# Two transformer layers on one core: VectorE's separate increments after its own writes are removed

## The reference

```python
x = layernorm(x + attn0(x))   # 16 heads of 8; q and k are divided by their row norms; softmax(q k / (8 * temperature)) v, projection
x = layernorm(x + ffn0(x))    # rows quantized to int8 by their absolute maximum, times int8 weights, scaled back, plus a bias
x = layernorm(x + attn1(x))   # 16 heads of 8; q and k normalized per head, rotated by position; causal softmax; projection
x = layernorm(x + ffn1(x))    # silu(x Wg) * (x Wu), times Wd, hidden size 384
```

## Time and profile before

| | us |
|---|---|
| median of 3 timed runs (lowest, highest) | 828.03 (827.97, 828.52) |
| span of the profiled execution, first to last instruction | 825.0 |
| TensorE matmul busy in the span | 799.1 |
| ScalarE busy | 770.4 |
| VectorE busy | 537.4 |
| GpSimd busy | 169.6 |

### The profile page before, as it was taken

How to read it: one execution, slowest core, us unless ns; L and a number is a source line. 1 busy time by engine, 2 the same in 40 slices (tenths; PEclk the granted TensorE clock), 3 DMA queues, 4 the chain that set the end, 5 groups by cost and what they waited for, 6 DMA issues and landing times.

```text
span 825.0 us, 18937 instructions
## 1 busy us (share of the span) xinstructions
PE 799.1 (97%) x7465; PEld 298.2 (36%) x7465; DVE 537.4 (65%) x1426; ACT 770.4 (93%) x869; POOL 169.6 (21%) x370
## 2 busy tenths in 40 slices
PE   8999999999999999999999999999999999999996
PEld 4332333333333433333333433343333443443444
DVE  4353747858849678678953676774563467786656
ACT  4999999999999999999999999999999999899972
POOL 3110100100102501133100611023200354362210
PEclk9999999999999999999999999999999999999999
DMA  5766312324314712451340421331231231061000
GB/s 145 259 219 226 144 41 102 130 64 175 121 50 152 246 40 77 142 184 48 136 159 27 154 78 40 111 120 42 76 134 46 87 108 52 27 223 74 14 14 15
DMA packets 48557, 88.74 MB, mean 108 GB/s; under 512 B 5200, under 2 KB 14544, under 8 KB 48464
## 3 DMA queue, kind: packets, MB, share of 16 engines
q1 hardware_dynamic: 47696, 85.95, 30.7%
q0 software_dynamic: 288, 1.05, 0.4%
q10 hardware_dynamic: 480, 0.48, 0.2%
HBM read 50.50 MB, written 35.65 MB: 104 GB/s over the span
## 4 chain that ended last, share of the span: by engine, by line
PE 78%; DVE 14%; ACT 5%; issue 3%; POOL 0%; DMA 0%; ACTq 0%; DVEq 0%; POOLq 0%
PE ps L1019 37%; PE ps L997 23%; PE ps L887 9%; ACT probs L834 4%; PE ps L972 3%; PE ps L876 3%; DVE mid_y L1220 1%; PE ps L1053 1%; DVE th L1431 1%; DVE sums_t L1259 1%; DVE hT L1432 1%; DVE mid_st L1222 1%; DVE mid_part L1422 1%; DVE mid_part L1421 1%; PE ps L881 1%
## 5 line engine op out<-in xcount | busy, mean ns | idle before, releaser
L834 ACT ACTIVATE probs<-ps 128x1024 f32<-128x1024 f32 x800 | 747.7, 1051 | 26.9 <-PE ps L997 20.9
L1019 PE MATMUL ps<-probs,v_st 128*32 128x512 f32 (+3 forms) x3584 | 424.7, 556 | 3.2 <-issue 2.1
L997 PE MATMUL ps<-q_st,k_st 32*128 32x512 f32 (+3 forms) x1792 | 262.6, 458 | 2.3 <-ACT probs L834 1.6
L997 PEld LDWEIGHTS ps<-q_st,k_st 32*128 32x128 f32 x1792 | 122.5, 181 | 290.5 <-ACT probs L834 234.9
L742 POOL TENSOR_SCALAR_AFFINE_SELECT probs<-probs 128x256 f32<-128x256 f32 x256 | 105.8, 437 | 143.1 <-ACT probs L834 141.6
L1019 PEld LDWEIGHTS ps<-probs,v_st 128*32 128x32 f32 x3584 | 81.5, 108 | 112.9 <-issue 81.7
L710 POOL COPY v_st<-v_all 128x256 f32<-128x256 f32 (+1 forms) x65 | 26.2, 412 | 350.5 <-PE ps L1019 342.3
L1400 DVE COPY mid_qkv<-ps 128x384 f32<-128x384 f32 x32 | 17.8, 558 | 49.1 <-PE ps L887 48.1
L1259 DVE STREAM_TRANSPOSE sums_t<-ps 128x512 f32<-128x512 f32 x32 | 22.9, 716 | 35.8 <-PE ps L1019 35.1
L972 PE MATMUL ps<-yTp,w_hid 128*128 128x512 f32 x84 | 30.8, 448 | 4.0 <-DVE gate_sb L1426 2.5
L1400 DVE COPY prep_qkv<-ps 128x384 f32<-128x384 f32 x24 | 13.4, 558 | 26.0 <-PE ps L887 25.0
(11 more groups left out here) (190 smaller groups left out, 636.9 us busy)
## 6 DMA issues: line engine op xcount, KB each, us to landing
k_st<-parts_scratch SPq DMA_DIRECT2D x46, 512.0 KB, 3.5
parts_scratch<-mid_part SPq DMA_DIRECT2D x34, 512.0 KB, 3.9
q_st<-parts_scratch SPq DMA_DIRECT2D x62, 256.0 KB, 3.9
parts_scratch<-prep_part SPq DMA_DIRECT2D x28, 512.0 KB, 3.9
k_st<-parts_scratch SPq DMA_DIRECT2D x17, 256.0 KB, 2.9
xT<-in_xT SPq DMA_DIRECT2D x8, 256.0 KB, 4.0
x_all<-in_x SPq DMA_DIRECT2D x8, 256.0 KB, 6.3
out<-yo SPq DMA_DIRECT2D x7, 256.0 KB, 2.3
```

Source lines behind the costliest of these rows:

```text
L834: nc.scalar.activation(probs[:, k % PS, :, 0:w], slot(k)[:, :, 0:w], ACT.Exp).then_inc(probs_ready, 1)
L997: last_ = mm(slot(k)[:, e, at:at + n], k_st[row, p % KB, kt * P:(kt + 1) * P], q_st[row, p % KB, lo:HALF], start=True, stop=not shifted)
L1019: last_ = mm(acc[HR * h:HR * (h + 1), lo:HALF], v_st[:, p % VB, kt, h, :], probs[:, (2 * s + h // 2) % PS, h % 2, at:at + n], start=FIRST[ ...
```

## The change

VectorE's separate increments on the ten lines above go. In their place, either the last writing instruction itself raises the reader's semaphore (scaled and rotated q and k, layernorm outputs, rounded values), or the reader waits for the count `side_read` that the last reading instruction raises anyway (q, k, v copied, parts ready, gate copied). The chunks 0 and 1 of layer 0, whose data does not pass through the side bank, keep their semaphores. VectorE's wait for its own write in front of an increment goes too, except behind the last q, k, v copy, where the squares read what was just written. Pure renamings (`qkv_copied["prep"]` to `qkv_copied`, `parts_ready["prep"]` to `parts_ready`) are left out here.

```diff
     named = lambda what: {n: sem(f"{n}_{what}") for n in job}
-    qkv_copied = named("qkv_copied")
+    qkv_copied = sem("qkv_copied")
...
     qk_ready = named("qk_ready")
-    parts_ready = named("parts_ready")
+    parts_ready = sem("parts_ready")
...
     attn_ready, norm_ready = sem("attn_ready"), {n: sem(f"{n}_norm") for n in tok}
-    gate_copied, tanh_ready, out_ready, y_out = sem("gate_copied"), sem("tanh_ready"), sem("out_ready"), sem("y_out")
+    tanh_ready, out_ready, y_out = sem("tanh_ready"), sem("out_ready"), sem("y_out")
...
+    def wait_copied(eng, name, c):
+        if (name, c) in (("prep", 0), ("prep", 1)):
+            eng.wait_ge(qkv_copied, c + 1)
+        else:
+            eng.wait_ge(side_read, FILL[name, c, "qkv", TC - 1] + 1)
...
-        eng.wait_ge(parts_ready[name], c * 2 + (2 - u))
+        if (name, c) == ("prep", 0):
+            eng.wait_ge(parts_ready, 2 - u)
+        else:
+            eng.wait_ge(side_read, FILL[name, c, "qkT", u] + 1)
...
             if c >= 2:
-                sp.wait_ge(qkv_copied["prep"], c - 1)
+                wait_copied(sp, "prep", c - 2)
...
         far_scores = sp.value_load(far_any[0:1, 0:1], min_val=0, max_val=1)
-        sp.wait_ge(parts_ready["prep"], 3)
+        sp.wait_ge(side_read, FILL["prep", 1, "qkT", 1] + 1)
...
         def store_v(name, c):
-            pool.wait_ge(qkv_copied[name], c + 1)
+            wait_copied(pool, name, c)
...
         def tanh(c, j):
-            act.wait_ge(gate_copied, c * NJ + j + 1)
+            act.wait_ge(side_read, FILL["last", c, "gate", j] + 1)
...
-        def layernorm(name, what, src, dst):
+        def layernorm(name, what, src, dst, done=None):
...
                 for t in range(TC):
-                    ch.step(ts(dst[:, t, :], src[:, t, :], s_[:, 0, 2 * t:2 * t + 1], s_[:, 2, t:t + 1],
-                               ALU.subtract, ALU.mult))
-                ch.need()
+                    op = ts(dst[:, t, :], src[:, t, :], s_[:, 0, 2 * t:2 * t + 1], s_[:, 2, t:t + 1], ALU.subtract, ALU.mult)
+                    op.then_inc(done, 1) if done is not None and t == TC - 1 else ch.step(op)
+                if done is None:
+                    ch.need()
...
             elif what == "scale":
-                ch.link(tt(by(out[:] if name == "prep" else qk), by(qk), bc(per(1).unsqueeze(3), wide), ALU.mult))
+                op = tt(by(out[:] if name == "prep" else qk), by(qk), bc(per(1).unsqueeze(3), wide), ALU.mult)
                 if name == "prep":
-                    dve.sem_inc(qk_ready[name], 2)
+                    op.then_inc(qk_ready[name], 2)
+                else:
+                    ch.link(op)
...
                 u = 0 if what == "scale_q" else 1
-                ch.link(tt(out[:, :, u * C:(u + 1) * C], qk[:, :, u * C:(u + 1) * C],
-                           bc(per(1)[:, :, u].unsqueeze(2), [P, TC, C]), ALU.mult))
-                dve.sem_inc(qk_ready[name], 1)
+                tt(out[:, :, u * C:(u + 1) * C], qk[:, :, u * C:(u + 1) * C],
+                   bc(per(1)[:, :, u].unsqueeze(2), [P, TC, C]), ALU.mult).then_inc(qk_ready[name], 1)
...
             else:
-                ch.link(tt(by_u(out[:]), by_u(out[:]), table(2, slice(0, D)), ALU.add))
-                dve.sem_inc(qk_ready[name], 2)
+                tt(by_u(out[:]), by_u(out[:]), table(2, slice(0, D)), ALU.add).then_inc(qk_ready[name], 2)
...
                 if what == "ln_out":
-                    layernorm(ln, what, x_all[:, c], y1)
-                    if name == "last":
-                        dve.sem_inc(norm_ready[ln], 1)
+                    layernorm(ln, what, x_all[:, c], y1, norm_ready[ln] if name == "last" else None)
                 elif what == "ln_out_x":
-                    layernorm(ln, what, y2, x_all[:, c])
-                    dve.sem_inc(norm_ready[ln], 1)
+                    layernorm(ln, what, y2, x_all[:, c], norm_ready[ln])
...
                         dve.wait_ge(y_out, c * 16)
-                    layernorm(ln, what, y2, yo)
-                    dve.sem_inc(out_ready, 1)
+                    layernorm(ln, what, y2, yo, out_ready)
...
                     ch.link(ts(y2, y2, -128.0, MAGIC, ALU.max, ALU.add))
-                    ch.link(ts(xq[:], y2, -MAGIC, None, ALU.add))
-                    dve.sem_inc(xq_ready, 1)
+                    ts(xq[:], y2, -MAGIC, None, ALU.add).then_inc(xq_ready, 1)
...
                     got()
-                    dve.sem_inc(qkv_copied[name], 1)
...
                     tt(part[:, k, 1, :], side, part[:, k, 0, :].bitcast(F32), ALU.subtract).then_inc(side_read, 1)
-                got()
-                dve.sem_inc(parts_ready[name], 1)
...
                 v.tensor_copy(gate_sb[:, k % 2, :], side).then_inc(side_read, 1)
-                got()
-                dve.sem_inc(gate_copied, 1)
```

More of the change, by code:

```diff
@@ L619, in _ @@
         for u, dst in ((1, k_st), (0, q_st)):
-            sp.wait_ge(parts_ready["prep"], 2 - u)
+            sp.wait_ge(parts_ready, 2 - u)
             for y in range(PRODUCTS // 2):
@@ L744, in mask @@
                 op.then_inc(masked, 1)
-        pool.wait_ge(qkv_copied["prep"], 1)
+        pool.wait_ge(qkv_copied, 1)
         pool.sem_inc(v_stored["prep"], 1)
@@ L809, in head @@
                 square(0, t)
-            nc.scalar.activation(v_all[:, 0, 0, tiles_of(0), :], ps[:, 0:TC, 2 * C:3 * C], ACT.Copy).then_inc(qkv_copied["prep"], 1)
+            nc.scalar.activation(v_all[:, 0, 0, tiles_of(0), :], ps[:, 0:TC, 2 * C:3 * C], ACT.Copy).then_inc(qkv_copied, 1)
             for t in range(TC):
@@ L818, in head @@
                 nc.scalar.activation(buffers("prep", 1)["qkv"][:, t, :], ps[:, TC + t, 0:3 * C], ACT.Copy).then_inc(
-                    head_copied if t < TC - 1 else qkv_copied["prep"], 1)
+                    head_copied if t < TC - 1 else qkv_copied, 1)
             for u, dst in ((1, k_st), (0, q_st)):
-                act.wait_ge(parts_ready["prep"], 2 - u)
+                act.wait_ge(parts_ready, 2 - u)
                 for y in range(PRODUCTS // 2, PRODUCTS):
@@ L1068, in _ @@
             turn4(lambda t: job["prep"]["qk"][:, t, u * C:(u + 1) * C], head_bank[u], ident).then_inc(head_turned, 1)
-        pe.wait_ge(qkv_copied["prep"], 1)
+        pe.wait_ge(qkv_copied, 1)
         keep_warm(WARM[3], 0)
-        pe.wait_ge(qkv_copied["prep"], 2)
+        pe.wait_ge(qkv_copied, 2)
         pe.wait_ge(flags_made, 1)
@@ L1080, in steps @@
                         stage(name, c, what, k)
-            pe.wait_ge(parts_ready["prep"], 2)
+            pe.wait_ge(parts_ready, 2)
             for k in range(SLOTS):
@@ L1474, in _ @@
                 rows_norm("prep", c, what)
-            dve.wait_ge(qkv_copied["prep"], c + 1)
+            dve.wait_ge(qkv_copied, c + 1)
             rows_norm("prep", c, "scale_k")
@@ L1482, in _ @@
                 ch.link(tt(part[:, 1, 1, :], head_bank[1], part[:, 1, 0, :].bitcast(F32), ALU.subtract))
-                dve.sem_inc(parts_ready["prep"], 1)
+                dve.sem_inc(parts_ready, 1)
                 dve.wait_ge(head_high, 1)
```

## The result

The changed kernel takes 820.84 us (median of 5, 820.54 to 822.96) against 828.03 (826.41 to 828.52) in runs beside it: ratio 0.9923, 95% interval 0.9912 to 0.9933. Two later sets of runs gave 821.17 (0.9918, 0.9905 to 0.9932) and 821.18 (0.9923, 0.9909 to 0.9936).

The account below looks back on a forecast made before the run. ScalarE and TensorE hold each other, with gaps where side-bank fills wait for VectorE. Waits and increments 2.95 us plus port order 1.33 (masks' 0.1 off) made 4.28; 825.0 - 4.28 + 3.03 = 823.8 us, range 822.4 to 827.0.

Parts of the forecast that it names:

- (a): Places where VectorE's wait and increment both go and VectorE goes on: 0.24 us each, eleven on the chain.
- (b): Last q, k, v copy (L1403), where only the increment goes and the wait stays: 0.11 us each, five on the chain.
- (c): Places where a reader on another engine is next and its semaphore rises earlier: 0.06 us each, four on the chain.
- (d): After q, k, v copies VectorE's square would start ahead of GpSimd's v copy: 0.44 us each, 1.43 in the sum.
- The 0.1 us for later masks: At 589 us, GpSimd's masks start later behind its v copy and TensorE's sums wait: 0.1 us taken off the gain.
- the slower rival: Layer 1: VectorE takes the port ahead of GpSimd's masks, TensorE's sums wait; 830.0 us with twelve masked steps; chance 0.08.
- the 93 that are not on the chain are costed at nothing: Of the 113 increments in the trace, those off the chain of waits were priced at zero.
- The caps at 186 to 200 and 250 to 262: Gain limited to TensorE's waits: 0.21 + 0.55 at 190.64 and 194.89, 0.55 at 257.63 us.
- with nothing capped: Upper bound on the gain, not limited by TensorE's waits: 5.63 us.
- GpSimd stays first: Rival: GpSimd's v copy still starts ahead of VectorE, so the square's gain and the masks' 0.1 go: 825.1 us; chance 0.22.
- the free wait: Rival: removing VectorE's wait gains nothing, only the readers' 0.06 us is left: 827.8 us; chance 0.12.
- another path that takes over early: Rival: TensorE's stream or the exponentials take over at most places, leaving 1.4 us: about 826.6 us; chance 0.08.

Follow-up runs that it names:

- the last writes alone: Kernel before, with only the last writes of scaled and rotated q and k, layernorm outputs and rounded values raising the reader's semaphore: 825.63 us, ratio 0.9977.
- the doubled: Kernel before, with a second increment, of a semaphore nobody reads, behind each of the 113: 829.58 us, ratio 1.0024.
- the kept ones: Changed kernel, with VectorE's wait for its own read put back behind parts and gate copies, without an increment: 822.67 us, ratio 0.9941.

## Why the prediction was wrong

**What bounds the kernel**: right. VectorE was late where the fills of the side bank waited for it, and what it won reached TensorE and ScalarE.

**The prices**: right but for one place. (a) 0.24 is 0.11 for the increment and 0.12 for the wait (0.146 to 0.034 to -0.083 us). (b) 0.11 likewise. (c) 0.06: 0.07 at 136 to 143 with the last writes alone, but 0.19 at 722 to 728, where VectorE's own next work was late too. The Trainium skill's sentence that "the semaphore costs nothing extra here" ("VectorE: DVE Perf Modes", section "The DRAIN you can't avoid"), said there of a semaphore after each of eight copies, doesn't hold for the waits and separate increments of this kernel: with it, (a) and (b) would have been zero, and the doubled and the kept ones would have changed nothing.

**The order of VectorE and GpSimd (d)**: right, with the size forecast: VectorE at 0.03 and GpSimd at 0.06 us behind the copy (before, 0.15 and 0.12), 1.66 to 1.22 us for the square in eight of eight, the copy of v at 1.67. I overlooked two squares of layer 0 that also stand right behind a copy (at 48.40 and 77.82 us); they went from 1.66 to 1.22 too and won nothing in the table. The 0.1 us for later masks was not there. In the step of the earlier trace rows the first mask now starts later, but the two masks end 2.4 us behind the copy's end as they did, since the first one had taken 1.40 us beside the long square and now takes 0.40. TensorE's weights wait 1.1 us for masks, in three places, before and after. That also settles the slower rival: the masks pay nothing that reaches TensorE.

**The sum**: this step failed first. It was short by 1.4 us, and more than half of that is the term "the 93 that are not on the chain are costed at nothing": 0.70 at 395 to 410 and 0.17 at 500 to 525. The caps at 186 to 200 and 250 to 262 were too low by 0.34 together: they were taken from the waits of matmuls (0.55 each at L1418), but the weights in front of those had waited 0.87 and 0.86 us for VectorE and now wait 0.25 and 0.24. The (c) at 722 to 728 adds 0.14. I followed the one chain and the waits of TensorE that were labelled with VectorE; a wait labelled "issue" (the 1.03 us at 400.10) was VectorE's as well, and at 500 to 525 the increments stood some operations ahead of the one that TensorE waited for. The bound "with nothing capped", 5.63, came within 0.1 of the 5.7 found, but by luck: the caps held to about 0.1 at all their places but 250 to 262, and other places were missing.

**The base**: this step failed too. "825.0 - 4.28 + 3.03" joined the span of one execution to the median of others that were about 1.0 us longer. What lies outside the span is 2.05 us, so the sum, as it stood, should have been 825.0 + 2.05 - 4.28 = 822.8. With 5.7 it gives 821.35 for an execution whose first square starts as late as in the profiled one; the changed kernel's runs without a fall are at 820.54 to 821.55. The 0.5 us that are left to the median of 820.84 are within what the start of the span varies by (1.05 us between two profiles of the changed kernel); why it varies was not looked into.

**The rivals**: GpSimd stays first, the free wait, another path that takes over early, and the masks each fell by their own signs: squares at 1.22, starts ahead of the write's end, 5.7 us instead of 1.4, masks' waits unchanged. ScalarE's gaps shrank by 4.2 us, as foreseen (about 4), and the 5.7 us also hold the head, the tail and gaps in front of other work.

## What to carry to other kernels

A separate increment behind a write cost VectorE twice here, once for the wait and once for the increment; if a count that the write raises anyway can serve the reader, take it. When a change makes an engine earlier everywhere, don't price only the places that one chain of waits names: go through every wait of the bounding engine, those marked "issue" too, and ask which read or write ended just before it. And subtract a gain from the profiled execution's own time: the median can be that of a longer execution, as here by 1.0 us.

## What the runs showed of the hardware

Where VectorE's square and GpSimd's copy waited for the same count, they started in a fixed order, ten times of ten in one trace: VectorE 0.03 us behind the end of the write and GpSimd 0.06. The one that starts 0.03 us later takes longer: 1.66 instead of 1.22 us for VectorE's square, 1.67 instead of 0.61 for GpSimd's copy. TensorE's granted clock fell to half for 3.4 us in six of the fourteen traces, at 696 to 704 us or at 747. Each time its matmuls had just waited 1.2 to 1.3 us for VectorE's gate copy, and the fall came 0.3 to 0.9 us behind the end of that wait. All fourteen traces have two such waits, at 695 to 703 and at 743 to 753 us, and six of these 28 were followed by a fall; whether the clock fell differed between executions of one program. By the mean clock the fall is in about two of five timed runs of the kernel before (median span longer by 0.8 us) and in three of fifteen of the changed one (longer by 1.4 to 2.4). The time outside the span was 2.0 to 2.2 us in all runs that list their span.
